# Giving every planned matmul piece of a scan layer a step of its own

## The reference, cut to what matters

```python
h = _ln(x, norm1_w, norm1_b) * (1.0 + s1) + sh1
# _mamba, forward and on the flipped sequence:
x, z = split(h @ in_proj_W); x = silu(conv4(x) + conv_b)
xdbl = x @ x_proj_W; dt = softplus(xdbl[..., :16] @ dt_proj_W + dt_proj_b)
hst = hst * exp(dt * A) + dt * B_t * x_t      # for every token
y = einsum('bdn,bn->bd', hst, C_t) + Dp * x
out = (y * silu(z)) @ out_proj_W
x = x + g1 * (fwd + bwd);  h = _ln(x, ...) * (1 + s2) + sh2
x = x + g2 * (silu(h @ w1) * (h @ w2)) @ w3
```

## Time and profile before

| | |
|---|---|
| median of 3 runs | 4430.45 us (4430.39 to 4430.64) |
| the profiled execution's own time | 4424.82 us |
| its span, first to last instruction | 4422.6 us |
| busy: PE, DVE, ACT, POOL | 93%, 90%, 88%, 83% |
| mean granted TensorE clock | 0.984 |
| scans of layer 1 | 297.6 us to about 1628.7 us |
| scans of layer 3 | behind 1980 us |

### The profile page before, as it was taken

How to read it: one execution, slowest core, us unless ns; L and a number is a source line. 1 busy time by engine, 2 the same in 40 slices (tenths; PEclk the granted TensorE clock), 3 DMA queues, 4 the chain that set the end, 5 groups by cost and what they waited for, 6 DMA issues and landing times.

```text
span 4422.6 us, 109586 instructions
## 1 busy us (share of the span) xinstructions
PE 4130.1 (93%) x45534; PEld 3202.6 (72%) x45534; DVE 3985.9 (90%) x3829; ACT 3884.1 (88%) x6090; POOL 3672.1 (83%) x1378
## 2 busy tenths in 40 slices
PE   8999899899899988999999999999999999999998
PEld 5457777677677764458878877778777778777777
DVE  5669999899899986759999999999999999999996
ACT  4569999999999964569999999999999999999995
POOL 3338998898889973349999999999999899999995
PEclk8999999999999999999999999999999999999999
DMA  4012221222121221022232422322422423323221
GB/s 169 1 24 68 59 70 63 57 60 68 59 59 66 66 79 41 1 44 83 86 74 82 87 69 81 84 72 85 86 75 70 87 81 95 66 79 70 75 80 40
DMA packets 241499, 305.16 MB, mean 69 GB/s; under 512 B 116448, under 2 KB 175712, under 8 KB 241008
## 3 DMA queue, kind: packets, MB, share of 16 engines
q1 hardware_dynamic: 241008, 298.15, 23.7%
HBM read 289.84 MB, written 8.26 MB: 67 GB/s over the span
## 4 chain that ended last, share of the span: by engine, by line
ACT 38%; PE 37%; DVE 16%; issue 7%; POOL 1%; DVEq 0%; DMA 0%; SPq 0%; ACTq 0%; POOLq 0%
ACT weights_c L1833 10%; PE psum L879 8%; DVE work L2344 8%; PE psum L1171 7%; ACT work L1850 7%; PE psum L1153 7%; ACT work L1833 7%; PE psum L1150 6%; ACT weights_c L1850 5%; PE psum L1298 5%; DVE weights_c L2344 5%; ACT L1517 2%; ACT modulation L1833 2%; PE psum L1381 1%; PE psum L1091 1%
## 5 line engine op out<-in xcount | busy, mean ns | idle before, releaser
L2783 POOL TENSOR_TENSOR work<-work,weights_a 128x2048 f32<-128x2048 f32 x512 | 1977.1, 3871 | 109.7 <-DVE work L2344 84.3
L2344 DVE TENSOR_TENSOR_SCAN work<-weights_c,psum 128x512 f32<-128x512 f32 x1316 | 1507.8, 1202 | 84.9 <-PE psum L1153 74.0
L2783 POOL TENSOR_TENSOR weights_c<-weights_c,weights_a 128x2048 f32<-128x2048 f32 x256 | 989.9, 3873 | 38.7 <-DVE weights_c L2344 38.1
L1153 PE MATMUL psum<-ident,work 128*128 128x128 f32 x5464 | 935.2, 274 | 12.5 <-ACT work L1850 4.3
L1833 ACT ACTIVATE work<-work,decay 128x504 f32<-128x504 f32 x1172 | 814.9, 706 | 45.4 <-DVE weights_c L2344 24.8
L1153 PEld LDWEIGHTS psum<-ident,work 128*128 128x128 f32 x5464 | 664.9, 142 | 60.1 <-issue 32.4
L1153 PE MATMUL psum<-ident,weights_c 128*128 128x128 f32 x3752 | 697.4, 276 | 0.0
L2344 DVE TENSOR_TENSOR_SCAN work<-work,psum 128x512 f32<-128x512 f32 x586 | 674.4, 1198 | 18.4 <-PE psum L1153 14.9
L2344 DVE TENSOR_TENSOR_SCAN weights_c<-work,psum 128x512 f32<-128x512 f32 x586 | 674.5, 1198 | 14.1 <-PE psum L1153 13.6
L1171 PE MATMUL psum<-ident,work 64*128 64x64 f32 x16800 | 660.3, 229 | 8.0 <-POOL work L2783 7.2
L1171 PEld LDWEIGHTS psum<-ident,work 64*128 64x128 f32 x16800 | 588.0, 140 | 97.0 <-issue 73.6
(11 more groups left out here) (232 smaller groups left out, 6597.4 us busy)
## 6 DMA issues: line engine op xcount, KB each, us to landing
weights_a<-c_rows SPq DMA_DIRECT2D x384, 512.0 KB, 3.7
work<-b_diagonals SPq DMA_DIRECT2D x240, 128.0 KB, 2.1
weights_c<-b_diagonals SPq DMA_DIRECT2D x112, 128.0 KB, 2.1
b_diagonals<-weights_c SPq DMA_DIRECT2D x1, 4096.0 KB, 18.2
weights_c<-in_L_cond_fwd_in_w SPq DMA_DIRECT2D x8, 512.0 KB, 5.6
weights_c<-in_L_cond_fwd_xproj_w SPq DMA_DIRECT2D x4, 1024.0 KB, 7.1
weights_c<-in_L_cond_bwd_in_w SPq DMA_DIRECT2D x8, 512.0 KB, 5.4
weights_c<-in_L_cond_bwd_xproj_w SPq DMA_DIRECT2D x4, 1024.0 KB, 7.1
```

The source lines that it names most:

```text
L1153: last = nc.tensor.transpose(PS[:, bank, t * P:(t + 1) * P], buf["scaled"][s % INPUTS][t][:, j * P:(j + 1) * P], IDENT[:, :])
L2344: v.tensor_tensor_scan(buf["ring"][s % RING][:, along, j], buf["decay"][q % DECAYS[l]][:, along], PS[:, 4 + q % LOOKAHEAD, along], 0.0, AL ...
L2783: g.tensor_tensor(state, state, row.unsqueeze(2).broadcast_to([P, T, DC]), ALU.mult).then_inc(ss["prod_ready"], 1)
```

## The change

`Plan` now works out all steps when it is made. It goes through the pieces in the order of the list and gives each the first step that is at least its nominal one and later than the step of the piece before it, and moves on by one where that is an addition's step. Before, each piece's step was worked out by itself, so that two or three pieces could share one. Nominal steps, the list of jobs, their gaps and the readers' distances are as before.

```diff
-        self.at, t, self.stride = {}, 0, stride
+        self.at, t = {}, 0
         for name, pieces, gap in jobs:
             self.at[name] = (t, pieces)
             t += (pieces - 1) * stride + 1 + gap
-        self.start = start
-        self.spread = min((end - start) / t, 1.3)
+        spread, step, self.step_of = min((end - start) / max(t, 1), 1.3), start - 1, {}
+        for name, pieces, gap in jobs:
+            for k in range(pieces):
+                step = max(step + 1, start + int((self.at[name][0] + k * stride) * spread))
+                if step % DC == ADDED_AT:
+                    step += 1
+                self.step_of[name, k] = step

     def piece(self, name, k):
-        step = self.start + int((self.at[name][0] + k * self.stride) * self.spread)
-        return step + 1 if step % DC == ADDED_AT else step
+        return self.step_of[name, k]
```

## The result

The changed kernel takes 4439.26 us (median of 11 runs, 4436.67 to 4444.38); the kernel before took 4427.96 us beside it (11 runs, 4422.81 to 4433.64). The ratio is 1.0027, with an interval of 1.0018 to 1.0036: 11.3 us slower, with 8 to 16 us inside the interval. The forecast was 4434 us with a range of 4425 to 4442. The time is in the range, but the loss is more than three times the +3.3 us of the sum, and most of the interval lies above the 0.2% up to which I called it "same".

What follows compares the result with a forecast made beforehand. The scans were taken to set the pace in layer 1's runs 0 to 7, all that can move. Terms summed to +3.3 us on the 4430.45 us median, giving 4434 us, range 4425 to 4442.

Steps and rivals of the forecast that it cites:

- Run 1, `scaled`: Layer 1, run 1: POOL's `scaled` falls behind the product of state 3, so DVE's `normed` waits longer; +3.8 us.
- The clock behind it: Run 1, behind the `normed` wait: longer PE idleness at the lowered clock delays scan inputs; +0.2 us.
- Runs 3 and 5, up0 to up2: Layer 1, steps 64 to 74: spread bc gains 1.3 us, later readers of up0 and up1 lose more; +0.75 us a run.
- I take 0 there: bc pieces of even runs and run 1, and run 0: PE equally late at the last piece; 0, bounds -1 and +1 us.
- Even runs, out0 and out1: Runs 2, 4, 6: out0's later reader makes PE wait 1.6 us before out1; +0.9 us a run, +2.7 for three.
- down0 and down1: Runs 3 and 5: spreading three pieces of step 87 shrinks DVE's and PE's waits; -2.2 us a run.
- Odd runs up to step 33: Runs 3 and 5, steps 3 to 31: gate0 waits for mean's later reader, mostly regained at var; +0.1 us a run.
- Run 7: Layer 1, run 7: spreading down0 spares most of one wait; -0.4 us.
- A: Rival: waits behind shared steps simply go, 30 us less the 3.8 of run 1; 4404 us, chance 0.09.
- B: Rival: PE's new bank waits drop the clock, slowing inputs and additions, 10.5 us for seven; 4444 us, chance 0.17.
- C: Rival: `scaled` in run 1 finds cover, gains and losses cancel, no change; 4430 us, chance 0.12.
- layer 3's stretch: Layer 3: its plans come out as before, so its stretch in the profile keeps the same length.

Runs made afterwards that it cites:

- e7: Kernel before with one edit: POOL's `scaled` of run 1 one step later, no piece moved; 4430.06 us, ratio 1.0014.
- e0: The kernel before, unchanged, profiled once more; 4425.19 us, ratio 0.9998.
- e4: Changed kernel, but bc's pieces keep their shared steps in runs 1, 3 and 5 of layer 1; 4431.44 us, ratio 1.0017.
- e9: Changed kernel, but var keeps its two pieces in one step in runs 2, 4 and 6 of layer 1; 4432.30 us, ratio 1.0015.
- e5: Kernel before, with only down0 and down1 of runs 3 and 5 of layer 1 spread, readers with them; 4421.00 us, ratio 0.9988.
- e8: Kernel before, with down0 and down1 of runs 3 and 5 and bc of runs 2, 4 and 6 spread, readers with them; 4420.32 us, ratio 0.9985.
- e2: Changed kernel's spread pieces, but readers with a distance over 0 placed by the old last step; 4442.96 us, ratio 1.0038 to before.
- e6: Changed kernel, but out0's pieces keep their shared steps in runs 2, 4 and 6 of layer 1; 4431.71 us, ratio 1.0016.

## Why the prediction was right in sign and small in size

*Run 1, `scaled`: right.* I gave DVE's wait as about 5.7 us and the loss as +3.8; the trace has 5.69 and 3.80, e7 has 5.60 and 3.76 with nothing else changed. The clock behind it, taken as +0.2, can't be read: the scan of 22 waits 0.84 us here and 0.76 in e7 against 0.34 in before, but 0.91 in e0, which is before unchanged. That run 1 is only 3.1 us longer (2.5 against e0) comes from waits at low clock at the scans of 46 and 62 of before (0.91 and 1.46 us), which are not in this execution, while bc adds.

*"Runs 3 and 5, up0 to up2", taken as +0.75 a run: this is the step that failed.* The stretch from scan 63 to 74 measured +2.4 and +2.9 us. The forecast's +0.75 held a gain of 1.3 us at the scan of 64 from the spread bc (measured: 1.15 and 1.13), and priced the rest by the readers on DVE alone. It left out ACT's copy of bc, which frees the bank. The copy moved from step 60 to 63 of a program that has no slack there, and up0 stood right behind it in 64: PE waited 1.18 and 2.24 us, and the scans between 64 and 70 fell 2.8 and 3.3 us behind. With bc shared (e4, in which up0 stays too) the stretch is +0.3 and +0.4 us. The term is short by 1.6 + 2.2 = 3.8 us, the larger part of the 4.7 us by which layer 1 is off the sum (8.0 - 3.3). Behind the scan of 70, where up1's reader acts, both kernels lose 0.75 us; that this equals the forecast's number is chance, since that one was the sum of a gain and of larger losses. "I take 0 there", said of the bc pieces of the even runs and of run 1, went by PE's work alone for the same reason. In run 1 the copy holds dt0 for 1.37 us, with 2.0 us at the scan of 72, but e4 shows that taking the wait away gives only 0.2 us net there.

*Even runs, out0 and out1: right in mechanism, mis-sized.* PE's wait is 1.65 us (I said 1.6) and the scans of 43 are 1.8 us late (1.4 by 44). bc and var give 0.8 back by 55 (0.5 in the forecast); what the walk didn't reach is the stretch behind, where by 59 another 1.2 us is lost in runs 4 and 6 and 0.5 in run 2. There PE's first piece of dt0 waits 1.07 us for `normed`, whose step follows var's, where before it waited 0.52 (in run 2 of before 1.19, because `normed` itself had waited 0.56 us for POOL's `scaled`). By the scan of 61 that is +1.6, +2.2 and +2.3 us in runs 2, 4 and 6 (in run 4 without the 1.0 us that before lost at scan 15), 6.1 us in all, against +0.9 a run in the sum. Only part of it is var's: e9 gets 0.5 us a run back. The lengths of the runs, +0.3, +1.3 and +1.3, add to 2.9, near my 2.7, but only because before had a wait of 0.9 us at low clock in each (scans 62, 15 and 122) that the changed kernel's execution hasn't. The agreement of the totals is luck.

*down0 and down1: right.* Forecast -2.2 a run, measured -2.0 in the changed kernel and in e5 and e8.

*Odd runs up to step 33:* +0.1 forecast, +0.1 in run 3 and +0.8 in run 5. *Run 7:* -0.4 forecast, +0.2 measured. *Run 0* is inside its own spread of 2.6 us. Between the scans of 33 and 63 runs 3 and 5 lose another 0.8 us each; e5, whose plan is that of before up to there, differs from before by -0.2 and +0.8 us over the same stretch, so this can't be put down to the change.

*The rivals.* A (the waits behind shared steps simply go) is wrong: e2, with spread pieces and no later readers, cut the scans' waits for PE by 15 us and added 23.7 us of waits before DVE's own readers. B named the size of the loss that came, for another reason than it gave: the clock doesn't fall at the new claims, and in layer 1's scans it stood at its lower level for 41 us, not more than the 55 us in both executions of before. Windows around the 1.65 us wait in run 2 (PE, PEld, DVE, ACT, POOL busy, PEclk, DMA share, GB/s):

```profile
666.00:668.00 2.00, 0.35 (x2) 0.27 (x2) 2.00 (x3) 2.00 (x5) 0.76 (x1) 1.00 0.64 217
668.00:670.00 2.00, 2.00 (x27) 1.35 (x28) 1.36 (x2) 2.00 (x4) 2.00 (x1) 1.00 0.13 45
```

and the addition behind it took 1.24 us, its length in the rows at the 2.4 GHz level. Around the longest claim, 2.24 us in run 5, the granted clock is 1.00 as well. In run 1, where DVE stood for 5.69 us, it did fall:

```profile
478.00:480.00 2.00, 0.00 (x0) 0.00 (x0) 1.43 (x2) 0.00 (x0) 0.47 (x1) 0.50 0.64 227
```

C, no change to the end, is excluded by the measured interval. That layer 3's stretch would keep its length can't be judged from one profile, with a spread of 13 us in the rest. *What stays open:* how much of the 11.3 us of the medians lies outside layer 1. The 8.0 to 8.6 us of layer 1 are enough for the lower part of the interval (8 us); the other 3 may be the rest's own variation, and nothing was run that separates it. The total in the forecast's range is in part luck, too: the sum was short by 8 us, and the range held it because its upper end had been set for rival B.

## What to carry to other kernels

When a plan moves a piece, follow every engine that frees its buffer, above all one that copies the buffer out behind a full program of its own: a buffer that is handed from job to job makes "first piece to reader to next first piece" one length, and spreading a job is a gain only where the next job starts late enough (here down0 and down1, 2.0 us a run) and a loss where it starts in the next step (up0 behind bc). Two pieces in one step need not cost anything (out0 in the even runs is 1.9 us better shared than spread), and an engine that works in coarse units turns one step into a whole unit (3.8 us for `scaled`). Taking back single jobs of a rule that loses as a whole can make it a gain (from +0.27% to -0.23%); how much of it one of the kept jobs brings by itself still has to be measured (here the down jobs, -0.12%).

## What the runs showed of the hardware

Code that is the same has a wait of 0.6 to 1.5 us in one execution and not in the other, and it is TensorE's clock in those looked at. It is so even between two executions of one kernel: at the scan of 15 in run 2 DVE doesn't wait in the first execution of before and waits 0.91 us in e0, where the granted clock was 0.55 just ahead (631 to 633 us). The scan of step 15 in run 4, kernel before:

```profile
991.27 1.22 DVE L2344 TENSOR_TENSOR_SCAN work<-weights_c,psum 128x512 f32<-128x512 f32 x1 [0.91 <-PE psum L1153]
```

and PE's windows ahead of it (columns as above), where the addition took 1.97 us:

```profile
988.00:989.00 1.00, 1.00 (x19) 1.00 (x20) 1.00 (x2) 1.00 (x3) 1.00 (x2) 0.50 0.84 266
989.00:990.00 1.00, 1.00 (x21) 0.88 (x17) 1.00 (x2) 1.00 (x2) 1.00 (x3) 0.50 0.68 234
```

In e5 the same step, with the same pieces, ran at the full clock, with an addition of 1.24 us and no wait:

```profile
979.00:980.00 1.00, 1.00 (x33) 0.93 (x29) 1.00 (x2) 1.00 (x3) 1.00 (x2) 1.00 0.76 238
```

In before PE had been busy for 0.57 of 2 us shortly ahead (984 to 986), with no idle stretch over 1.43 us; in e5 it was 0.57 of 2 us as well (975 to 977), and the clock stayed. The Trainium skill (TensorE: Matmul & The Clock Gate, Why this matters for your kernels) says that gaps without matmuls bring the half rate. The traces agree in part: this lull did it in one execution and not in another, and the waits of 1.65 and 2.24 us above didn't do it. Such a wait is as large as most terms of this study, so the run lengths had to be read step by step, and lengths alone would have given even runs and e6 a wrong verdict.
